# The second layer's routed experts: from gathering and adding expert outputs to scattering weighted rows onto the output

## What is computed

```python
def _moe_forward(x, Wr, br, W1, b1, W2, b2):      # x: (3750, 512); 8 experts, 512 -> 256 -> 512
    logits = xf @ Wr.T + br
    routing = jax.nn.softmax(logits, axis=-1)
    sel_w, sel_idx = jax.lax.top_k(routing, TOP_K)          # TOP_K = 2
    sel_w = sel_w / jnp.sum(sel_w, axis=-1, keepdims=True)
    combine = jnp.zeros((N, E)).at[jnp.arange(N)[:, None], sel_idx].add(sel_w)
    h = jax.nn.gelu(jnp.einsum('nd,edf->enf', xf, W1) + b1[:, None, :])
    y = jnp.einsum('enf,efd->end', h, W2) + b2[:, None, :]
    return jnp.einsum('ne,end->nd', combine, y)

x = x + _L1_ffn_ref(_layernorm(x)[None], ...)[0]            # this x is the output
```

## Time and profile before

| | us |
|---|---|
| median of three runs | 3759.92 |
| lowest and highest of the three | 3759.78, 3761.09 |
| profiled execution, its own time | 3758.3 |
| profiled execution, span of the trace | 3756.2 |
| of the span: experts stage, 3366.4 to 3659.6 | 293.2 |
| of the span: combining stage, 3659.6 to the end | 96.6 |
| TensorE busy over the span | 2888.8 (77%) |

### The profile page before, as it was taken

How to read it: one execution, slowest core, us unless ns; L and a number is a source line. 1 busy time by engine, 2 the same in 40 slices (tenths; PEclk the granted TensorE clock), 3 DMA queues, 4 the chain that set the end, 5 groups by cost and what they waited for, 6 DMA issues and landing times. The chain is left out here.

```text
span 3756.2 us, 37939 instructions
## 1 busy us (share of the span) xinstructions
PE 2888.8 (77%) x9194; PEld 1384.6 (37%) x9195; DVE 2188.7 (58%) x3514; ACT 572.3 (15%) x968; POOL 1623.5 (43%) x1595
## 2 busy tenths in 40 slices
PE   5989548999877881599996799908989986549990
PEld 2444212222223550355552345503223221536660
DVE  5779786666655767532221405596666664964444
ACT  2100110000004640011110210011000000512110
POOL 0776037777760000144442177206777772002216
PEclk9999769999998875699998899959999998559995
DMA  4345227777761121155554527306777773143337
GB/s 155 88 97 119 80 80 210 210 211 210 210 177 47 69 83 50 34 156 145 141 141 115 122 85 163 101 0 182 210 210 210 210 210 97 63 162 120 129 103 249
DMA packets 330788, 512.22 MB, mean 136 GB/s; under 512 B 172499, under 2 KB 178115, under 8 KB 329999
## 3 DMA queue, kind: packets, MB, share of 16 engines
q0 software_dynamic: 113824, 311.79, 30.6%
q1 hardware_dynamic: 92975, 194.62, 14.7%
q10 hardware_dynamic: 123840, 3.94, 1.9%
HBM read 423.29 MB, written 86.92 MB: 136 GB/s over the span
## 5 line engine op out<-in xcount | busy, mean ns | idle before, releaser
L1011 PE MATMUL bank<-aggregate_zg,aggregate_onehot 128*128 x2112 | 1094.3, 635 | 159.4 <-issue 121.3
L949 POOL DMA_INDIRECT aggregate_zg<-z_rows,src_groups x940 | 891.4, 948 | 651.5 <-POOLq L2207 330.9
L990 DVE TENSOR_TENSOR aggregate_zg<-aggregate_zg,bank 128x1024 f32<-128x1024 f32 x470 | 573.7, 1221 | 468.5 <-DMA aggregate_zg<-z_rows,src_groups 468.0
L1011 PEld LDWEIGHTS bank<-aggregate_zg,aggregate_onehot 128*128 128x128 f32 x2112 | 347.1, 191 | 905.3 <-issue 899.0
L376 POOL DMA_INDIRECT front_d<-src_scores,src_chunks x320 | 324.2, 1013 | 186.8 <-issue 97.3
L1619 POOL DMA_INDIRECT exp_xg<-hn_rows,exp_gather_tok x64 | 71.6, 1118 | 537.3 <-DVE exp_gather_tok L1681 415.8
L672 PE MATMUL bank<-front_w,front_table 128*120 128x512 bf16 x960 | 244.4, 392 | 27.5 <-DVE front_w L549 27.5
L1763 PE MATMUL bank<-exp_w,exp_h_t 128*117 128x512 f32 x512 | 225.7, 595 | 0.7 <-ACT exp_h_t L1710 0.7
L935 ACT COPY acc<-bank 128x512 f32<-128x512 f32 x60 | 35.2, 586 | 1192.5 <-PE bank L1011 1192.5
L970 DVE TENSOR_TENSOR aggregate_onehot<-bank,columns 128x256 f32<-128x256 f32 x528 | 215.3, 416 | 0.0
L1630 POOL DMA_INDIRECT x_rows<-exp_y,exp_add_tok x64 | 137.0, 2141 | 164.8 <-DVE exp_y L1672 129.6
(11 more groups left out here) (390 smaller groups left out, 3517.6 us busy)
## 6 DMA issues: line engine op xcount, KB each, us to landing
exp_w<-in_L_ffn_w SPq DMA_DIRECT2D x32, 1024.0 KB, 7.6
slot_out<-exp_y SPq DMA_DIRECT2D x66, 256.0 KB, 2.0
z_rows<-front_z SPq DMA_DIRECT2D x60, 256.0 KB, 2.0
hn_rows<-fin_xn SPq DMA_DIRECT2D x20, 768.0 KB, 3.5
aggregate_zg<-z_rows,src_groups POOLq DMA_INDIRECT x940, 3.7
front_early<-src_key SPq DMA_DIRECT2D x16, 640.0 KB, 4.1
front_early<-src_tile SPq DMA_DIRECT2D x16, 640.0 KB
front_edge<-src_key SPq DMA_DIRECT2D x16, 640.0 KB, 3.9
```

The lines of the kernel that those rows point to most:

```text
L949: pool.indirect_dma_start(zg[:, r, j, :], None, k.z_rows[:, :], bass.IndirectOffsetOnAxis(k.src_groups[:, n:n + 1], 0)).then_inc(gathered[ ...
L990: v.tensor_tensor(z, z, bcast_last(scales[:, at:at + J * H], DH), ALU.mult).then_inc(msg_ready, 1)
L1011: mm = nc.tensor.matmul(k.banks[:, bass.ds(bank, 1), :].rearrange("p a n -> p (a n)"), onehot[:, n % RING, j, :], zg[:, bass.ds(at, 1), j, ...
```

## The change

The combining stage is gone, with its buffers, and so are `slot_out`, its zero rows and the 66 stores of `y`. In their place:

- The finishing stage stores, behind each block of `xn`, also the block of `k.x` in the output. The rows of `xn` go to a new tensor `routed_rows` whose rows have 520 columns: 512 of `xn` and 8 for the token's weight for each expert.
- The routing stage computes these 8 weights (`combine`, three operations on 128x240 elements) and ScalarE stores them in `routed_rows` (3840 x 32 bytes). It also computes `slot_rows`, the output row of every slot (an empty slot gets a spare row of its own behind the 3750 real ones), and `scatter_after`, for every tile the number of the first tile of its expert. `token_slots` is no longer written.
- In the experts stage a gather brings 520 columns. It waits for `x_t_ready` and no longer for `turned`, since VectorE now copies the 8 weights out of the buffer (`gates`) ahead of its copy of the transposed tile. VectorE picks the column of the tile's expert (`gate`), ScalarE multiplies `y` by it, and POOL scatters the tile with addition onto the output. SP counts finished scatters in `landed`.
- Ahead of a scatter POOL reads `scatter_after` into a register and waits until `landed` has reached it, so that rows of one expert are added only when all of the experts before it have landed. VectorE waits for `landed` before it writes the same `y` buffer again, where it had waited for the store.

The core of the diff:

```diff
 finish_layer1, SP
-                    sp.dma_start(k.hn_rows.rearrange("(i j p) d -> i p j d", j=TB, p=P)[n], xn[:, :, :]).then_inc(xn_stored, 16)
+                    sp.dma_start(blocks(k.routed_rows[:, 0:D])[n], xn[:, :, :]).then_inc(xn_stored, 16)
+                    sp.dma_start(blocks(k.out[0:NPAD])[n], k.x[:, n * TB:(n + 1) * TB, :]).then_inc(x_stored, 16)
 route1, DVE and ACT
+                v.tensor_tensor(tmp[:, :, :], oh[:, 0], bcast_last(k.weights[:, :, 0], E1), ALU.mult)
+                chain(v.tensor_tensor(combine[:, :, :], oh[:, 1], bcast_last(k.weights[:, :, 1], E1), ALU.mult))
+                v.tensor_tensor(combine[:, :, :], combine[:, :, :], tmp[:, :, :], ALU.add).then_inc(combine_ready, 1)
                 dve.wait_ge(from_pe, 1)
...
                 chain(v.tensor_copy(k.tile_expert[:, :], te[0:1, :]))
+                v.memset(begins[:, 0, 0:1], 0.0)
+                chain(v.tensor_tensor(begins[:, 0, 1:], te[0:1, 1:], te[0:1, 0:MT - 1], ALU.not_equal))
+                chain(v.tensor_tensor(begins[:, 0, :], begins[:, 0, :], k.iota[0:1, 0:MT], ALU.mult))
+                chain(v.tensor_tensor_scan(begins[:, 1, :], begins[:, 0, :], begins[:, 0, :], 0.0, ALU.max, ALU.max))
+                v.tensor_scalar(k.scatter_after[:, :], begins[:, 1, :], float(TB), None, ALU.add)
...
+                act.dma_start(k.routed_rows[:, D:].rearrange("(t p) e -> p t e", p=P), combine[:, :, :]).then_inc(combine_stored, 16)
 experts1, SP
-                    for j in range(TB):
-                        sp.wait_ge(y_done, i * TB + (j + 1 + TB))
-                        sp.dma_start(rows[i * TB + j], y[:, j, :]).then_inc(y_stored, 16)
-                    sp.wait_ge(y_stored, i * (16 * TB) + 16 * TB)
-                    sp.sem_inc(y_free, TB)
+                    for j in range(TB):
+                        sp.wait_ge(added[j], i * 16 + 16)
+                        sp.sem_inc(landed, 1)
 experts1, POOL
-                for n in range(MT):
-                    if n >= TB:
-                        pool.wait_ge(turned, n + 1)
-                    pool.indirect_dma_start(xin[:, n % TB, :], None, k.hn_rows[:, :],
+                def gather(n):
+                    pool.indirect_dma_start(xin[:, n % TB, :], None, k.routed_rows[:, :],
                                             bass.IndirectOffsetOnAxis(k.slot_tokens[:, n:n + 1], 0)).then_inc(x_loaded[n % TB], 16)
+
+                def scatter(n):
+                    wait_here(pool, landed, pool.value_load(k.scatter_after[0:1, n:n + 1], min_val=TB, max_val=MT + TB), passed)
+                    pool.wait_ge(y_scaled, TB + n + 1)
+                    pool.indirect_dma_start(k.out[:, :], bass.IndirectOffsetOnAxis(k.slot_rows[:, n:n + 1], 0),
+                                            y[:, n % TB, :], None, compute_op=ALU.add).then_inc(added[n % TB], 16)
+
+                for n in range(TB):
+                    gather(n)
+                for i in range(R):
+                    for n in range(i * TB + TB, min(MT, i * TB + (TB if i else 2 * TB) + (TB if i else 0))):
+                        pool.wait_ge(x_t_ready, n + 1)
+                        gather(n)
+                    for j in range(TB):
+                        scatter(i * TB + j)
 experts1, DVE
+                        v.tensor_copy(gates[:, j, :], xin[:, j, D:])
                         v.tensor_copy(x_t[:, j, :, :].rearrange("p c n -> p (c n)"), k.ps[j][:, :]).then_inc(x_t_ready, 1)
...
+                    dve.wait_ge(y_scaled, i * TB + TB)
+                    for j in range(TB):
+                        ins = v.tensor_copy(gate[:, j:j + 1], gates[:, j, bass.ds(expert[j], 1)])
+                    ins.then_inc(gate_ready, 1)
                     if not last:
+                        dve.wait_ge(gate_ready, i + 1)
                         take(i + 1)
                     for j in range(TB):
                         dve.wait_ge(y_ready, i * TB + (j + 1))
-                        dve.wait_ge(y_free, i * TB + (j + 1))
+                        dve.wait_ge(landed, i * TB + (j + 1))
 experts1, ACT
+                    act.wait_ge(gate_ready, i + 1)
+                    for j in range(TB):
+                        act.wait_ge(y_done, i * TB + (j + 1 + TB))
+                        nc.scalar.activation(y[:, j, :], y[:, j, :], ACT.Copy, scale=gate[:, j:j + 1]).then_inc(y_scaled, 1)
```

More of the change, by code:

```diff
@@ L1333, in _ @@
                 sp.dma_start(gw[:, :, :], I["L1_ffn_WrT"].rearrange("(c p) n -> p c n", p=P)).then_inc(loaded, 16)
-                sp.wait_ge(zeroed, 1)
-                sp.dma_start(k.slot_out[MT * P:].rearrange("(c p) d -> p c d", p=P), zeros.unsqueeze(1).to_broadcast([P, 2, D])).then_inc(zero_stored, 16)
+                blocks = lambda rows: rows.rearrange("(i j p) d -> i p j d", j=TB, p=P)
                 for n in range(NB):
                     sp.wait_ge(xn_ready, n + 1)
-                    sp.dma_start(k.hn_rows.rearrange("(i j p) d -> i p j d", j=TB, p=P)[n], xn[:, :, :]).then_inc(xn_stored, 16)
-                sp.wait_ge(zero_stored, 16)
+                    sp.dma_start(blocks(k.routed_rows[:, 0:D])[n], xn[:, :, :]).then_inc(xn_stored, 16)
+                    sp.dma_start(blocks(k.out[0:NPAD])[n], k.x[:, n * TB:(n + 1) * TB, :]).then_inc(x_stored, 16)
                 sp.wait_ge(xn_stored, 16 * NB)
-            @block.gpsimd
-            def _(pool):
-                nc.gpsimd.memset(zeros, 0.0).then_inc(zeroed, 1)
+                sp.wait_ge(x_stored, 16 * NB)
             @block.vector
@@ L1820, in route1 @@
         tile_at = sb("tile_at", [P, MT], F32)
+        spare_row = sb("spare_row", [P, MT], F32)
+        combine = sb("combine", [P, NT, E1], F32)
+        begins = sb("begins", [1, 2, MT], F32)
         te = sb("te", [P, MT], F32)
@@ L1975, in experts1 @@
         y = sb("y", [P, TB, D], F32)
-        turned, x_t_ready, g_ready, h_ready, gelu_done, h_turned, h_t_ready, y_ready, y_done, y_free, y_stored, passed = (
+        gates = sb("gates", [P, TB, E1], F32)
+        gate = sb("gate", [P, TB], F32)
+        turned, x_t_ready, g_ready, h_ready, gelu_done, h_turned, h_t_ready, y_ready, y_done, gate_ready, y_scaled, landed, passed = (
             sem(n) for n in ("turned", "x_t_ready", "g_ready", "h_ready", "gelu_done", "h_turned", "h_t_ready",
-                             "y_ready", "y_done", "y_free", "y_stored", "passed"))
+                             "y_ready", "y_done", "gate_ready", "y_scaled", "landed", "passed"))
+        added = [sem(f"added{j}") for j in range(TB)]
         x_loaded = [sem(f"x_loaded{j}") for j in range(TB)]
@@ L2092, in routed_experts @@
         k.weights_loaded = nc.alloc_semaphore(name="weights_loaded")
+        k.slot_rows = ctx.enter_context(nc.sbuf_tensor("exp1_slot_rows", [P, MT], I32))
+        k.scatter_after = ctx.enter_context(nc.sbuf_tensor("exp1_scatter_after", [1, MT], I32))
         route1(k, I)
         experts1(k, I)
[L2097 to L2147 removed]
@@ L2165, in build @@
         k.hn_rows = dram("hn_rows", (NPAD, D))
-        k.slot_out = dram("slot_out", ((MT + 2) * P, D))
+        k.routed_rows = dram("routed_rows", (NPAD, D + E1))
+        k.out = out
         k.x = sb("x", [P, NT, D], F32)
@@ L2222, in build @@
                 stage(routed_experts, I)
-                stage(combine1, out)
 def kernel(**inputs):
```

82 lines of the change are left out of this document (20 added, 62 removed).

## The result

The changed kernel takes 3832.64 us (median of 4 executions, 3830.4 to 3836.03), the kernel before, beside it, 3759.85. The ratio is 1.0196, with a 95% interval of 1.0178 to 1.0214: slower by 73 us. The forecast was 3825, with a range of 3772 to 3895.

A forecast was written before the change was run, and what follows sets the result against it. TensorE bounds the experts stage now; with the change, gathers behind late scatters on POOL lengthen rounds. 3758.3 - 91 + 0 + 2 + 132 + 21 = 3822 us; with the median 1.6 above the profiled run, 3824, said as 3825; range 3772 to 3895.

The forecast's parts named there:

- The combining stage: End of the kernel: 99.9 us behind the last addition become 8.4, saving 91 us, between 88 and 93.
- The finishing stage: Ten more stores on SP's queue land under TensorE's last logits: cost 0, without that cover 1 us.
- The routing stage: Weight operations fit within a VectorE wait; small chained operations for `scatter_after` and `slot_rows` add 2 us, 1 to 3.
- The round: Experts stage: gathers queued behind late scatters on POOL lengthen it from 12.69 to 19.3 us; 20 rounds, +132 us.
- the clock: Experts stage: TensorE's granted clock falls while it is idle, net +1.4 us a round, 0 to 2.5.
- The landing behind scatters: Experts stage: gathers land after 3.5 us; landing later, at 4.6, could add 0 to 1.1, taken as 0.
- the register read: On POOL before scatters: hidden under the scatter before, taken as 0; if not, +1.4 us a round.
- The expert changes: Five scatters wait on `landed` for the expert before, +4.2 us each, +21 us in all, 16 to 25.
- Cheap scatters: Rival: a scatter costs POOL no more than a gather, round 15.6 us, total 3740; chance 0.10, hidden case included.
- One by one: Rival: each scatter waits for the one before to land, round 26.2 us, total 3940; chance 0.06 with anything beyond 3895.
- All hidden: Rival: scatters hide entirely, round stays 12.69 us, total 3670 to 3690; within the 0.10 for faster.
- the Trainium skill's rule: GpSimd transfers take 2.0 us plus bytes over 436 GB/s, generation small: 3785 by landing alone, near 3665 with both.

The follow-up runs named there:

- gap filled: Changed kernel with five unread multiplications each round between TensorE's first product and the transposes that wait for gathers: 3816.14 us, ratio 1.0154.
- plain scatters: Changed kernel with scatters that write and don't add, so the output is wrong: 3777.59 us, ratio 1.0048.
- kernel without scatters: Changed kernel with each scatter replaced by a plain count behind the same waits for scaled tiles, without the wait on `landed`: ratios 0.995 and 0.9967 in two runs.
- run without the guard: Changed kernel with every slot scattered to its own spare row, and the read of `scatter_after` and wait on `landed` left out: 3806.0 us, ratio 1.0129.
- gathers first: Changed kernel with GpSimd issuing gathers one round earlier, ahead of the scatters they used to follow, nothing left out: 3675.48 us, ratio 0.9777.

## Why the prediction was right, step by step

**The combining stage** was to save 91 us. The end of the last addition to the end of the span is now 3834.3 - 3825.08 = 9.2 us, against 99.9: 90.7 saved. The last three rows of GpSimd and VectorE:

```profile
3824.39 0.69 DVE L2056 TENSOR_TENSOR exp_y<-bank,exp_b 128x512 f32<-128x512 f32 x1 [1.02 <-PE bank L2106]
3824.53 1.55 POOL L2014 DMA_INDIRECT out_x<-exp_y,exp_slot_rows  x1 [0.30 <-issue]
...
3826.39 1.55 POOL L2014 DMA_INDIRECT out_x<-exp_y,exp_slot_rows  x1 [0.30 <-issue]
```

The sum was right by luck, since its parts were not. The last scatter stood half a microsecond behind its scaled tile, since GpSimd was still at the one before; at the median landing of 5.0 us, where 5.9 was taken, it was in at about 3831.4; and the end took 2.9 us from there, where 1.7 was the estimate.

**The finishing stage** was to cost nothing: it takes 142.4 us, with the ten new stores in it, and took 142.3 before. **The routing stage** was to cost 2 us: it takes 48.7 us and took 47.6 before, so 1.1. The new work did go into the wait of the earlier trace rows, which shrank from 2.06 to 1.07 us:

```profile
3344.99 0.66 DVE L1895 TENSOR_TENSOR_SCAN route_incl<-route_keep,bank 128x240 f32<-128x240 f32 x1 [1.07 <-PE bank L1964]
```

**The round** was to be 17.9 us and 1.4 for the clock, 19.3 in all. The starts of the first product give fourteen ordinary rounds of 18.3 to 20.2 us with a mean of 19.45. Its single steps, from the round above:

| step, from T | predicted | measured |
|---|---|---|
| scatters start | -0.3, +1.6, +3.5 | -0.55, +1.37, +3.25 |
| gathers start | +5.3, +6.6, +7.8 | +5.11, +6.43, +7.72 |
| third transpose ends | +11.8 | +12.85 |
| from there to the next T | 6.04, and 1.4 net for the clock | 6.66 |

The means over the fourteen ordinary rounds, and over those of the kernel with the gap filled, part the clock from the rest:

| from T, us | predicted, clock apart | gap filled | changed kernel |
|---|---|---|---|
| third gather starts | 7.8 | 7.7 | 7.4 |
| third gather lands | 11.3 | 11.4 | 11.3 |
| third transpose ends | 11.8 | 12.2 | 12.8 |
| from there to the next T | 6.04 | 6.04 | 6.68 |
| round | 17.9 | 18.25 | 19.45 |

The mechanism is the one predicted. Two terms of the sum were mis-sized, by little and to opposite sides, and that the total came so near is luck in part. At full clock the round is 18.25 us and not 17.9. The landing behind scatters was taken as 3.5 us, with the rise to 4.6 put at zero; the median is 4.2 over all gathers, but 3.9 for the third, on which the round hangs (3.75 with the gap filled), and its transposes are done 0.8 us behind its landing and not 0.5. The run with plain scatters has 3.5 over all at the same place in the queue, so it is the addition in the transfers ahead that delays them, and not the place. The clock was taken as 1.4 us a round, and the filled gap takes back 1.2. It doesn't work quite as the prediction had it, which saw only the second product slowed: 0.6 to 0.7 us lie already in the transposes before that product, which end 1.4 us behind the third landing in place of 0.8, and as much behind them, 6.68 us against 6.04; 0.3 comes back as gathers that start earlier, and the landing is 0.15 longer. In the kernel without scatters a fall cost 1.4 us from one kind of round to the other, by their middle values of 16.9 and 15.5. The duration of a scatter, 1.58, and the register read at 0, the bound that might have added 1.4 us a round, were both right. The last interval was 21.1 us and not an ordinary one: the gathers of the last round landed after 6.2 to 6.8 us. Their tiles hold no pairs, so all their rows are the same one. That was in no term; it is 1.7 us. The trace of before had the sign of it: its last three gathers landed after 4.0, 4.1 and 4.6 us, and the 4.6 that the prediction read in the earlier trace rows as the slowest landing is one of them and not an ordinary gather.

**The expert changes** were to cost 4.2 us each, 21 in all. The five rounds of 23.4 to 24.0 us lie 4.1 above the others, the trace shows 20.9 us of waits, and the run without the guard gives 22.5.

**The sum.** 132 and 21 make 153 for the rounds, where the stretch grew by 158.6: 5.6 more, of which ordinary rounds hold 20 x 0.15 = 3, the last interval 1.7 and the first one, at 15.53 in place of 14.53, 1. From the first gather to the last addition the stage grew by 158.9. So the stages of the change are -90.7 + 0.1 + 1.1 + 158.9 = +69.4 us in the pair of profiles, where the forecast was +64; with the 8.7 of the stages ahead that is the 78.1 of the two spans. The medians are 73 us apart on the chips of the first runs and 68 on those of the last, which is the +69.4 within the spread of the stages ahead.

**The rivals.** Cheap scatters gave 3740 on the assumption of 0.95 us of GpSimd. The plain scatters cost just that, 0.975, and gave 3777.6: the mechanism exists, but most rounds with them are 17 to 19 us and not 15.6. Three steps of that rival fell short: the gathers landed after 3.5 us, the third ones after 3.7, and not 3.1; the scatters waited 46 times for a scaled tile, which are ready some 1.7 us apart and not 1.25; and the granted clock was 0.87 over that stage and not full. Its place beside the kernel before, ratio 1.0048, is on the slower side after all. "One by one" didn't occur, as 39 gaps of 0.30 us show. "All hidden", 3670 to 3690, is what the experiment with the gathers first brings about, at 3675.5: the number was right for another order than the change has.

Of the Trainium skill's rule ("DMA: Bandwidth & Descriptors", section "Anatomy of one DMA — SWDGE (gpsimd) path"), 2.0 us plus bytes over 436 GB/s, the landing holds for one kind of transfer of this kernel only. It gives 2.6 us for 256 KB; a plain scatter landed after 2.7, a gather after 3.5, a scatter with addition after 5.0. Its statement that descriptor generation is small isn't borne out by any run here, if GpSimd's busy time is that generation: 0.94 to 1.65 us for each transfer of 128 rows. This time of three scatters is a part of what separates a round of 19.45 us from one of 15.5 to 16.9.

## What to carry to other kernels

Before a stage is folded into a loop that has room, follow the in-order queue that takes its instructions: what matters is not its busy share (37% here) but whether an instruction that can start only at the round's end stands ahead of one that the next round needs early. Put the prefetches ahead of the results of the same queue, by one buffer's depth, and the same added work costs nothing (3675 us against 3833). And where the engine in front then waits, count its clock as well: a few us of idle time a round cost it one more.

## What the runs showed of the hardware

- A scatter with addition of 128 rows of 2 KB costs GpSimd 1.58 us and lands after 5.0; the same without addition 0.98 and 2.7. Gathers issued behind additions land after 4.2 us, behind plain scatters after 3.5 (medians; by place in the round 4.9, 4.2, 3.9 against 3.3, 3.5, 3.7).
- GpSimd's read of a register and its wait on it, between two indirect transfers, cost nothing: the gap is 0.30 us with and without them.
- Extra multiplications in TensorE's idle time made the kernel faster, by 16.5 us, through the granted clock (0.96 in place of 0.83 to 0.84 over the stretch).
- The kernel without scatters had rounds at full clock and rounds at 0.90 side by side, with the same 2.1 to 2.6 us of TensorE's idle time in both, and a stretch that differed by 7 us between two executions. What decides between them is open.
- The last three gathers, whose 128 rows are all the same row, landed late in the traces of both orders and of before: after 4.0 to 4.6 us in the kernel before (median of all 3.5), 3.8 to 4.7 behind plain scatters (3.5), 4.7 to 5.7 with the gathers first, and 6.2 to 6.8 in the changed kernel (4.2). They are also the last of the stage in each, and the same rows at another place were not tried.
